# A four-layer network on one core: attention's early tiles rearranged, and the experts' gate and up product with the weights as stationary operand

## What is computed

```python
x = layernorm(x + L0_attn(x))   # rotary lightning attention, 16 heads of 32, chunks of 128 tokens, a running state
x = layernorm(x + L0_ffn(x))    # int8 weights, silu(gate) * up, 2048 wide
x = layernorm(x + L1_attn(x))   # q * cumsum(k * v) * sigmoid(g)
x = layernorm(x + L1_ffn(x))    # 32 experts, each token has 8 choices with rerouting

def expert_step(y, params):     # of the last layer
    wgu, wd, cw = params
    gu = x @ wgu.T              # 512 -> 2 * 192
    g, u = jnp.split(gu, 2, axis=-1)
    h = jax.nn.silu(g) * u
    y = y + h @ wd.T * cw[:, None]
```

## Time and profile before

| | |
|---|---|
| three timed runs | 1563.08, 1562.61, 1558.29 us, median 1562.61 |
| the profiled execution | 1556.97 us, of which the span from first to last instruction is 1555.1 |
| mean granted TensorE clock | 0.954 |
| busy | PE 90%, PEld 50%, DVE 58%, ACT 43%, POOL 49% |
| instructions | PE 10327 matmuls, 31694 in all |
| chain that ended last | PE 73%, DVE 13%, DMA 5%, issue 2% |
| of it by line | L889 20%, L910 11%, L716 7%, L722 6%, L739 6%, L598 6%, L880 5%, L899 2% |

### The profile page before, as it was taken

The page is one execution under the profiler, slowest core; times in us unless marked ns, Lnnn a source line. Parts: engine busy times, 40 slices in busy tenths (PEclk is TensorE's granted clock), DMA queues, the critical chain, the costliest instruction groups (busy, mean ns, idle before and its releaser), DMA issues.

```text
span 1555.1 us, 31694 instructions
## 1 busy us (share of the span) xinstructions
PE 1405.1 (90%) x10327; PEld 771.1 (50%) x10328; DVE 909.7 (58%) x1826; ACT 662.7 (43%) x1250; POOL 763.6 (49%) x691
## 2 busy tenths in 40 slices
PE   5799899799999999999886359999999999999990
PEld 2455555444444444445443226666666666666650
DVE  7677566676757676635988864444444444444435
ACT  6332222455454545423444424444444444444443
POOL 3565454510100101233645446777777677777655
PEclk9999999899999999999998569999999999999995
DMA  8777666689696969432303636888888988776767
GB/s 273 170 156 187 120 111 122 150 297 311 223 295 224 299 229 297 169 107 82 83 18 100 200 120 121 174 172 199 192 192 175 207 188 191 142 113 90 177 80 230
DMA packets 213452, 271.72 MB, mean 175 GB/s; under 512 B 133993, under 2 KB 135561, under 8 KB 212368
## 3 DMA queue, kind: packets, MB, share of 16 engines
q1 hardware_dynamic: 177776, 211.40, 46.6%
q0 software_dynamic: 35616, 59.58, 23.5%
HBM read 158.92 MB, written 101.71 MB: 168 GB/s over the span
## 4 chain that ended last, share of the span: by engine, by line
PE 73%; DVE 13%; DMA 5%; issue 2%; ACT 2%; POOL 2%; SPq 2%; DVEq 0%; ACTq 0%; POOLq 0%
PE bank L889 20%; PE bank L910 11%; PE bank L716 7%; PE bank L722 6%; PE bank L739 6%; PE bank L598 6%; PE bank L880 5%; PE bank L606 4%; DMA ARENA<-ARENA 4%; PE bank L673 2%; PE bank L899 2%; DVE ARENA L1251 1%; PE bank L818 1%; DVE bs L956 1%; DVE WA L1197 1%
## 5 line engine op out<-in xcount | busy, mean ns | idle before, releaser
L889 PE MATMUL bank<-ARENA,XT 128*128 x1908 | 364.0, 327 | 2.5 <-issue 1.4
L1801 POOL DMA_INDIRECT accs<-X,WA x159 | 252.3, 1587 | 89.6 <-issue 42.0
L889 PEld LDWEIGHTS bank<-ARENA,XT 128*128 128x128 f16 x1908 | 180.4, 98 | 124.5 <-issue 8.5
L1341 DVE COPY XT<-bank 128x1024 f16<-128x1024 f16 x159 | 110.0, 692 | 179.0 <-PE bank L880 146.2
L1794 POOL DMA_INDIRECT XT<-x_rows,WA x159 | 166.6, 1048 | 97.1 <-issue 42.1
L910 PE MATMUL bank<-ARENA,XT 128*128 x795 | 197.4, 379 | 0.8 <-issue 0.7
L1380 ACT ACTIVATE ARENA<-ARENA 128x512 f16<-128x512 f32 (+2 forms) x128 | 89.2, 708 | 231.7 <-DVE ARENA L1099 130.6
L1619 ACT ACTIVATE XT<-bank 128x192 f32<-128x192 f32 x159 | 52.5, 330 | 286.7 <-PE bank L889 232.7
L598 PE MATMUL bank<-XT,STG 128*128 128x512 f16 x640 | 152.4, 386 | 7.7 <-DVE ARENA L1145 7.6
L1647 POOL TENSOR_TENSOR rstd<-mv,mhalf 128x1 f32<-128x1 f32 x28 | 5.7, 202 | 281.9 <-DVE mv L959 281.9
L606 PE MATMUL bank<-WA,XT 128*128 128x512 f16 x540 | 126.2, 384 | 0.0
(11 more groups left out here) (244 smaller groups left out, 2184.6 us busy)
## 6 DMA issues: line engine op xcount, KB each, us to landing
w_scratch<-WA SPq DMA_DIRECT2D x64, 640.0 KB, 3.9
ARENA<-w_scratch SPq DMA_DIRECT2D x64, 640.0 KB
ARENA<-w_exp SPq DMA_DIRECT2D x48, 640.0 KB, 5.3
WA<-w_exp SPq DMA_DIRECT2D x16, 640.0 KB, 5.0
ARENA<-ARENA SPq DMA_DIRECT2D x32, 256.0 KB, 3.5
accs<-ARENA SPq DMA_DIRECT2D x20, 256.0 KB, 3.4
X<-x SPq DMA_DIRECT2D x4, 1024.0 KB, 6.8
ARENA<-wc SPq DMA_DIRECT2D x8, 512.0 KB, 6.0
```

The lines of the kernel that those rows point to most:

```text
L889: mm = pe.matmul(d, xTb[k.u % 2][:, a * KD + kd, :], weights(sl, b, kd * 2 * DFF, 2 * DFF), start=(a, b, kd) == (0, 0, 0), stop=(a, b, kd) ...
L1341: dve.tensor_copy(xTb[k.u % 2].rearrange("p c n -> p (c n)"), bank[k.u % 2][:, :].bitcast(F16)).then_inc(xt_sb, 1)
L1801: pool.indirect_dma_start(accs, bass.IndirectOffsetOnAxis(blkout[:, i:i + 1], 0), yD[i % 8], None, compute_op=ALU.add).then_inc(y_out[i % ...
```

## The change

Attention. On PE, tile 0 projects q of tile 1 before `to_state(0)`. On DVE, `angles(2)`, `angles(3)` and the pieces 8 and 9 go to later points of tiles 0 and 1. On ACT and POOL, the pieces from `LATE` on go behind k's halves and one tile later. On SP, each `turn(n)` is followed by one load instead of preceded by several, and the second layer's weights are spread over turns 9 to 11.

Experts. `gate_up` takes the weights as stationary side, 128 columns at a time, and the gathered x moves, 128 columns. It is called for three parts, each twelve matmuls: gate 0 to 127; gate 128 to 191 with up 0 to 63; up 64 to 191. The result has the features on the partitions, so that `h_transposes`, `ht_evac` and their buffers go away, and `expert_down` takes block k-2. DVE's product becomes three, on 64 partitions each; the combine weight moves to the scale of y's evacuation (`cwS`).

```diff
--- before.py
+++ after.py
...
@@ -413,35 +413,30 @@
...
-            sp.wait_ge(w_split, len(w_pieces))
-            sp.wait_ge(x_split, 2)
-            load_x(1)
             load_piece(12)
-            xt_move(1, 0, hlA, None)
-            turn(3)
-            load_piece(13)
-            load_x(2)
-            xt_move(2, 1, hlA, 16 * 1)
-            turn(4)
-            load_piece(14)
-            load_x(3)
-            xt_move(3, 2, hlA, 16 * 2)
-            turn(5)
-            load_piece(15)
-            xt_move(4, 3, hlA, 16 * 3)
-            turn(6)
-            xt_move(5, 4, hlA, 16 * 4)
-            turn(7)
-            sp.wait_ge(x_split, len(x_pieces))
-            for w, name in enumerate(("w_gate", "w_up", "w_down")):
-                sp.dma_start(raw8w[:, 4 * w:4 * w + 4, :], ins[name]).then_inc(b_raw, 16)
-            sp.dma_start(s_gateT, ins["s_gate"]).then_inc(b_small, 16)
-            sp.dma_start(s_upT, ins["s_up"]).then_inc(b_small, 16)
-            with sp.Fori(8, NT + 1) as n:
+            for n in range(3, 13):
+                xt_move(n - 2, n - 3, hlA, 16 * (n - 3) if n > 3 else None)
+                turn(n)
+                if n == 3:
+                    sp.wait_ge(w_split, len(w_pieces))
+                    sp.wait_ge(x_split, 2)
+                    load_x(1)
+                elif n < 7:
+                    load_piece(n + 9)
+                elif n < 9:
+                    load_x(n - 5)
+                    sp.wait_ge(x_split, len(x_pieces))
+                elif n < 12:
+                    sp.dma_start(*raws[n - 9]).then_inc(b_raw, 16)
+                else:
+                    sp.dma_start(s_gateT, ins["s_gate"]).then_inc(b_small, 16)
+                    sp.dma_start(s_upT, ins["s_up"]).then_inc(b_small, 16)
+            with sp.Fori(13, NT + 1) as n:
                 xt_move(n - 2, n - 3, hlA, None)
                 turn(n)
 
...
@@ -676,9 +671,13 @@
             def attention(t, first, last):
                 if not first:
                     out_proj(t - 1)
+                if first:
+                    pe.wait_ge(q_mul, 1)
+                    proj(t + 1, 0).then_inc(q_ready, 1)
                 to_state(t)
                 if not last:
-                    proj(t + 1, 0).then_inc(q_ready, 1)
+                    if not first:
+                        proj(t + 1, 0).then_inc(q_ready, 1)
                     pe.wait_ge(state_ready, t + 1)
                     proj(t + 1, 1).then_inc(k_ready, 1)
...
@@ -883,24 +882,16 @@
             def weights(sl, j, c0, n):
                 return Wslot[:, bass.ds(sl * (2 * WCOLS) + (j * WCOLS + c0), n)]
 
-            def gate_up(k, sl, some):
-                d = bank[2 + k.u % 2][:, 0:2 * DFF]
+            def gate_up(k, sl, part, some):
+                d = bank[2 + k.u % 2][:, part * P:(part + 1) * P]
                 for a, b, kd in some:
-                    mm = pe.matmul(d, xTb[k.u % 2][:, a * KD + kd, :], weights(sl, b, kd * 2 * DFF, 2 * DFF),
+                    w = weights(sl, b, kd * 2 * DFF + part * P, P)
+                    mm = pe.matmul(d, w, xTb[k.u % 2][:, a * KD + kd, :],
                                    start=(a, b, kd) == (0, 0, 0), stop=(a, b, kd) == (1, 0, KD - 1))
                 return mm
 
-            def h_transposes(k):
+            def expert_down(k, sl):
                 pe.wait_ge(h_lo, k.i + 1)
-                if not k.before(2):
-                    pe.wait_ge(ht_sb, k.i - 1)
-                d = bank[4 + k.u % 2][:, :].bitcast(F16)
-                for c in range(3):
-                    mm = pe.transpose(d[:, c * P:(c + 1) * P], hB[k.u % 2][:, c * P:(c + 1) * P], ident16[:, :])
-                mm.then_inc(ht_ready, 1)
-
-            def expert_down(k, sl):
-                pe.wait_ge(ht_sb, k.i + 1)
                 if not k.before(2):
                     pe.wait_ge(y_sb, k.i - 1)
...
@@ -917,32 +908,27 @@
                 if fresh:
                     held["packs"] = load_words(pe.engine, k, 0, 1)
                 e = expert_of(held["packs"], k.u)
-                if not k.before(3):
-                    expert_down(k.at(-3), expert_of(held["packs"], k.u - 3) % NSLOT)
+                if not k.before(2):
+                    expert_down(k.at(-2), expert_of(held["packs"], k.u - 2) % NSLOT)
                 sl = e % NSLOT
                 pe.wait_ge(w_in, e * 32 + 32)
                 pe.wait_ge(xt_sb, k.i + 1)
                 if not k.before(2):
                     pe.wait_ge(h_ready, k.i - 1)
-                gate_up(k, sl, products[:6])
+                gate_up(k, sl, 0, products)
                 if k.u == 2:
                     held["packs"] = held["packs"] + load_words(pe.engine, k, 1, 2)
-                gate_up(k, sl, products[6:8])
+                gate_up(k, sl, 1, products)
                 if not last:
                     gather_transposes(k.at(1))
-                gate_up(k, sl, products[8:]).then_inc(gu_ready, 1)
-                if not k.before(1):
-                    h_transposes(k.at(-1))
+                gate_up(k, sl, 2, products).then_inc(gu_ready, 1)
 
             pe.wait_ge(tables_ready, 1)
             pe.wait_ge(region_sb, 1)
             gather_transposes(Blk(0, 0, 8))
...
@@ -1038,19 +1023,20 @@
                 own.did(dve.scalar_tensor_tensor(state, state, kp, decS.unsqueeze(2).to_broadcast([P, PAIRS, HD]), ALU.mult, ALU.mult))
                 own.settle()
                 if first:
-                    split_piece(8)
+                    rotate(t + 1, 0)
                 else:
                     residual_a(t - 1)
                     norm_a(t - 1)
                 dve.wait_ge(kv_ready, t + 1)
                 dve.scalar_tensor_tensor(st, bank[1][:, 0:PAIRS * HD], kp, st, ALU.mult, ALU.add).then_inc(state_ready, 1)
                 if first:
-                    split_piece(9)
+                    angles(2)
+                    split_piece(8)
                 else:
                     ln_apply(t - 1, tile(t - 1), resA, 0)
-                if not last:
-                    rotate(t + 1, 0)
-                else:
+                    if not last:
+                        rotate(t + 1, 0)
+                if last:
                     dve.wait_ge(b_raw, 16 * 3)
...
@@ -1069,14 +1055,17 @@
                 dve.tensor_tensor(oL, oT, oH, ALU.subtract).then_inc(o_lo, 1)
                 dve.wait_ge(state_hi, t + 1)
                 dve.tensor_tensor(stateL, state, stateH, ALU.subtract).then_inc(state_lo, 1)
+                if isinstance(t, int) and t == 1:
+                    angles(3)
 
             attention(0, True, False)
             dve.wait_ge(x_in, 16)
-            for t in range(1, TB):
+            for t in range(1, TB + 1):
                 attention(t, False, False)
-            dve.wait_ge(x_in, 16 * BATCH)
...
@@ -1346,12 +1337,15 @@
                 if fresh:
                     mine["packs"] = load_words(dve.engine, k, 0, 2)
                 cw = xg[k.u % NG].bitcast(F32)[:, DIM:XROW][:, bass.ds(expert_of(mine["packs"], k.u), 1)]
-                h, split = h32[k.u % 2], hB[k.u % 2]
+                d, sg, h, turned = bank[2 + k.u % 2], sgD[k.u % 2], h32[k.u % 2], hT[k.u % 2]
+                dve.tensor_scalar(cwS[:, k.u % 8:k.u % 8 + 1], cw, 1 / (WS * WS), None, ALU.mult)
                 dve.wait_ge(sg_ready, k.i + 1)
-                dve.scalar_tensor_tensor(h, bank[2 + k.u % 2][:, DFF:2 * DFF], cw, sgD[k.u % 2], ALU.mult, ALU.mult).then_inc(h_ready, 1)
+                dve.tensor_tensor(h[0:64, 0:P], d[64:128, P:2 * P], sg[0:64, 0:P], ALU.mult)
+                dve.tensor_tensor(h[64:128, 0:P], d[0:64, 2 * P:3 * P], sg[64:128, 0:P], ALU.mult)
+                dve.tensor_tensor(h[0:64, P:2 * P], d[64:128, 2 * P:3 * P], sg[0:64, P:2 * P], ALU.mult).then_inc(h_ready, 1)
                 dve.wait_ge(h_hi, k.i + 1)
-                dve.tensor_tensor(split[:, 0:P], h[:, 0:P], split[:, P:2 * P], ALU.subtract)
-                dve.tensor_tensor(split[:, 2 * P + 64:3 * P], h[:, P:DFF], split[:, 2 * P:2 * P + 64], ALU.subtract).then_inc(h_lo, 1)
+                dve.tensor_tensor(turned[:, 0, :], h[:, 0:P], turned[:, 1, :], ALU.subtract)
+                dve.tensor_tensor(turned[64:128, 2, :], h[0:64, P:2 * P], turned[0:64, 2, :], ALU.subtract).then_inc(h_lo, 1)
 
             xt_evac(Blk(0, 0, 8))
             every_block(dve, 8, expert_block, 8)
...
@@ -1448,24 +1444,23 @@
                     convert(1)
                 else:
                     q_high(t + 1)
-                if isinstance(t, int) and LATE + t < NPA:
-                    hi_piece(LATE + t)
+                if first:
+                    turns(3)
+                    sines(2)
+                    k_high(t + 1)
                 act.wait_ge(state_ready, t + 1)
                 act.wait_ge(qa_free, t + 2)
                 copy(stateH, state).then_inc(state_hi, 1)
                 if last:
                     convert(2)
-                else:
+                elif not first:
```

(32 more changed lines are left out.)

40 lines of the change are left out of this document (22 added, 18 removed).

## The result

The changed kernel takes 1716.02 us (median; 1715.69 to 1716.71) against 1562.84 us before, a ratio of 1.0987 with a 95% interval of 1.0973 to 1.1001. Its profiled execution took 1716.7 us with a span of 1714.9 us, at a mean granted clock of 0.959 (0.954 before). The forecast was 1712 us.

What follows compares the result with a forecast made beforehand. PE's engine binds before; its sequencer, working out 24 addresses a block, binds after. 1556.97 (profiled execution) + 164 for experts - 15 for attention = 1706, with 5.6 for the median 1712 us; 1645 to 1770 in 8 of 10.

Steps and rivals of the forecast that it cites:

- The bound before: Expert stage: engine PE binds at 3.67 us a block; its sequencer's lap is 2.7 us, 1 us less.
- The engine's lap after, 3.54 us: Expert block on PE: 3.64 + 0.07 for 36 short matmuls at 0.056 us - 0.17 for `h_transposes`.
- The sequencer's lap after, 4.7 us: Expert block: sixteen added addresses at 0.125 us make PE's sequencer the bound; the stage costs 164 us more.
- The sign that I had given for it: Expert block: 24 addresses 0.12 to 0.13 us apart, 36 matmuls in groups of eight at that distance, then four close together.
- The wait for h: `expert_down` one block nearer to h: no wait at 4.7 us, 0.4 reserve at 3.54; rival with 5 us chain, chance 0.04.
- my 3.1 us: Experts: chain from a block's last `gate_up` through silu, products, high half, low halves and five handoffs.
- my rival with the engine as bound, 1532 us: Experts: an added address costs the sequencer under 0.05 us, so the stage gains 16 us; chance 0.08.
- Attention, -15 us: Attention tiles: three items gain 12 to 16 us together, bounds 5 and 20, taken as 15.
- The three items: Attention: earlier q projection up to 3 us, moved `angles(3)` 4 to 5, later splits and weight loads 5 to 8.
- the angles: Tile 1 on DVE: `angles(3)` moved from between the output's halves to behind `state_lo`, 4 to 5 us.
- the other two: Attention: q of tile 1 projected before `to_state(0)`, up to 3 us; splits and second-layer loads moved, 5 to 8.
- the settled tile's own work: Attention: after the three items, what is late next is this work on PE, which nothing in the change shortens.

Runs made afterwards that it cites:

- cut192: Kernel before with each product's 384 moving columns cut in two of 192 (16 addresses, 40 pairs a block): 1607.2 us, ratio 1.0294.
- share8_lag3: share8 with the down product of block i-3 instead of i-2 at the head of block i: 1571.6 us, ratio 1.0068.
- share8: Changed kernel with three column parts reading the same 128 weight columns (8 addresses, 36 short pairs kept, output of other weights): 1638.3 us, ratio 1.0479.
- after_lag3: Changed kernel with the down product of block i-3 instead of i-2 at the head of block i: 1714.6 us, ratio 1.0985.
- att_only: Kernel before with attention's half of the change alone, experts as before: 1555.1 us against 1560.0, ratio 0.9965.
- fix_both: att_only with SyncE's wait for all splits moved to tile 9, PE's split waits finer and behind output projection and `to_state`: 1541.95 us, ratio 0.9873.
- split_early: fix_both with ScalarE's and GpSimd's handling of the pieces of x one tile earlier, at the tile's end: 1540.9 us, ratio 0.9872.

## Why the prediction was right, and where it was wrong

**The bound before.** Right: with 16 addresses and 40 pairs in place of 8 and 28 the usual block stays at the engine's 3.67 us (cut192), so before the change the sequencer was well inside that.

**The engine's lap after, 3.54 us.** Right to the hundredth, seen only where the sequencer doesn't bind (share8_lag3). A short pair is 0.056 us on the engine with the weights as stationary side too. share8_lag3 loads the same 128 columns for all three parts, but the changed kernel, with the right ones, has more than half of its starts at that distance as well. The Trainium skill's 81 ns per pair at 128 columns (TensorE: Matmul & The Clock Gate, Back-to-back issue gap) is not borne out. An estimate by it, 44 pairs and 1.08 us for the five long matmuls, is 4.64 us, which happens to be the changed kernel's mean lap. Its average of 0.082 us a pair would have let one believe that; the single starts, at 0.056 or 0.124, and share8_lag3, with as many pairs and fewer addresses, tell the two apart.

**The sequencer's lap after, 4.7 us.** Right in size (4.64), +160.5 against +164, and in cause: 24 addresses, 0.124 us apart; with 16 of them taken away and the lead given back, 3.54. The sign that I had given for it, eight at that distance and then four close together, came out in its size but not in its form: in the block at 1205.43 four or five distances in each of the first two parts are 0.124 us and the others 0.056, and in the third part, behind the transposes, all but one are 0.056 or 0.063. Its two parts, 4.4 from the rows of one block and 0.3 on average for reads and branch, are the usual 4.4 and the lumps. The average was good where the sequencer binds all the time; with a little lead it is not, as cut192 shows.

**The wait for h.** I had said that at an engine lap of 3.54 a reserve of 0.4 us would be left. share8 shows that this reserve is not enough: the sequencer stands at the wait and starts the next block's addresses without a lead, 67 us. The way to h itself was no longer than my 3.1 us: from the end of the last `gate_up` matmul to the end of L1348 it took 2.7 us (median in share8). In the changed kernel itself it played no part (after_lag3). So my rival with the engine as bound, 1532 us, is not reached even with 8 addresses: share8 gives 1638, share8_lag3 1572. What addresses that cost nothing would give, no run shows.

**Attention, -15 us.** Wrong: -0.7 in this profile, -4.9 in att_only. The three items together do what they were to do: fix_both starts the scores of tile 8 15.4 us earlier than before: 1.9 at tile 0, 0.4 from there to tile 1, 5.4 to tile 2 and 7.7 over the six tiles to tile 8. Of the three, only the angles were tested alone: 4.6 us in their interval, within my 4 to 5. The shares of the other two, up to 3 and 5 to 8, stay unmeasured. The step that failed is the sentence that nothing but the settled tile's own work is late next, and that SyncE's moved loads end in time. I had costed the moved loads and the moved splits and not the waits that stand behind and before them. With the splits a tile later, PE's wait ahead of tile 3 costs 4.4 us (the interval from tile 2 to 3 is 20.6 in place of 16.2) and the two waits at tile 7 cost 6.9 (23.2 in place of 16.3): 11.3 of 15. Another 3 us went to the clock.

**The sum.** 1706 for the profiled execution; less 3.5 (experts) and plus 14.3 (attention) is 1716.8, against 1716.7. That the forecast of 1712 is only 4 us off is partly luck. For the profiled execution I was 10.7 us too low, and the 5.6 us that I added because the median lay that far above it did not come back: after the change the median is 0.7 below the profiled execution.

fix_both, which has the old experts, and split_early are faster than both kernels: 1.3% under the kernel before.

## What to carry to other kernels

Cost a matmul with a run-time address twice: on the engine by its columns, and on the sequencer that works the address out. Cutting matmuls into shorter ones multiplies addresses, and no busy share warns of it; what does is "issue" before the weight loads. An average of the sequencer's work is not enough either: a loop's turn or a wait on fresh data takes away its lead, and what was hidden comes out. When work that signals a semaphore is moved later, list each wait on it, with what is queued behind that wait, before counting the gain.

## What the runs showed of the hardware

- A pair with its address instruction passes PE's sequencer in 0.124 us, though the instruction lasts 46 ns. Without one it is next to nothing: in share8 the sequencer goes from the last address of a block at 1202.4 to its wait ahead of the transposes (L876) at 1202.6 past 17 pairs, some 0.01 us each. It reaches `expert_down` only at 1203.7, but that is the wait for h, whose last part (L1348) ends at 1203.58:

```profile
L889 PEldq FUSED_REGOPS  x8: 46/46/91, 1201.4 to 1202.4; - x8
...
L876 PEldq EVENT_SEMAPHORE  x1: 51/51/51, 1202.6 to 1202.6; - x1
...
1203.25 0.33 DVE L1348 TENSOR_TENSOR XT<-XT 64x128 f16<-64x128 f32 x1
...
L901 PEldq FUSED_REGOPS  x4: 46/46/192, 1203.7 to 1204.3; - x4
```

- The turn of an eight-block loop costs it 1.4 us, with one read of a word and its decoding (changed kernel, 1226.0 to 1227.4).
- The same stretch of code takes 617.4 to 623.2 us in fourteen profiles, by where its 32 to 37 us of half clock fall.
